# Layer-0 attention: squarings as 64x64 quadrant tiles, and the corner of the inverse made one stage early

## The reference, cut to what matters

```python
def step(Sm, inp):
    q_, k_, v_, g_, b_ = inp
    Sm = Sm * jnp.exp(g_)[..., None, None]
    kv = jnp.einsum('bhk,bhkv->bhv', k_, Sm)
    delta = (v_ - kv) * b_[..., None]
    Sm = Sm + jnp.einsum('bhk,bhv->bhkv', k_, delta)
    o = jnp.einsum('bhk,bhkv->bhv', q_, Sm)
    return (Sm, o)
```

## Time and profile before

| | |
|---|---|
| runs, us | 6044.46, 6041.1, 6032.09 (median 6041.1) |
| the profiled execution's own time, us | 6044.46 |
| span of the profile, us | 6046.2 |
| PE busy | 5221.5 us, 86% |
| DVE busy | 3480.2 us, 58% |
| ACT busy | 3055.8 us, 51% |
| POOL busy | 1178.3 us, 19% |
| squarings, L684 (five rounds of six) | 701.5 us busy on PE, 5120 records |

### The profile page before, as it was taken

One profiled execution on the slowest core, in us unless ns is written; L12 is line 12 of the kernel. 1 busy time (PEld: TensorE's weight loads), 2 busy tenths in 40 slices (PEclk: granted clock), 3 DMA queues, 4 the chain that ended last, 5 costly groups with the idle time before them and its releaser, 6 DMA issues. The chain is left out here.

```text
span 6046.2 us, 91895 instructions
## 1 busy us (share of the span) xinstructions
PE 5221.5 (86%) x32318; PEld 3893.8 (64%) x32318; DVE 3480.2 (58%) x6531; ACT 3055.8 (51%) x8923; POOL 1178.3 (19%) x1352
## 2 busy tenths in 40 slices
PE   5799999999989999989999699899998597399969
PEld 4477777877877778877887555555555354255545
DVE  3466666676666667666766566555552554543331
ACT  2466666666656666666666344344441244325421
POOL 0222222322222222222232100011110321002210
...
GB/s 85 19 19 17 13 19 19 18 17 17 19 19 13 17 19 19 17 14 19 22 19 13 46 1 1 65 1 0 0 0 20 27 1 13 21 1 1 1 21 14
DMA packets 51094, 103.57 MB, mean 17 GB/s; under 512 B 12848, under 2 KB 20176, under 8 KB 49520
## 3 DMA queue, kind: packets, MB, share of 16 engines
...
## 5 line engine op out<-in xcount | busy, mean ns | idle before, releaser
L896 ACT ACTIVATE dh_pb<-bank 64x128 f32<-64x128 f32 x3072 | 831.4, 271 | 272.5 <-PE bank L670 239.3
L684 PE MATMUL bank<-dh_cw,dh_pb 128*128 128x128 f32 x5120 | 701.5, 281 | 113.0 <-ACT dh_pb L896 111.4
L684 PEld LDWEIGHTS bank<-dh_cw,dh_pb 128*128 128x128 f32 x5120 | 635.5, 193 | 191.1 <-ACT dh_pb L896 164.4
L1034 DVE SCALAR_TENSOR_TENSOR dh_kq<-bank,dh_conv_kq,dh_kq 128x511 f32<-128x511 f32 (+2 forms) x408 | 305.4, 749 | 184.8 <-ACT dh_kq L853 173.6
L902 ACT ACTIVATE dh_cw<-bank 128x256 f32<-128x256 f32 x640 | 244.9, 385 | 255.1 <-PE bank L684 247.9
L621 PE MATMUL bank<-hT,dh_w_kq 128*128 128x512 f32 x544 | 276.7, 633 | 83.2 <-DVE dh_kq L1034 75.3
L1034 DVE SCALAR_TENSOR_TENSOR dh_v<-bank,dh_conv_v,dh_v 128x511 f32<-128x511 f32 (+2 forms) x384 | 284.2, 747 | 91.3 <-ACT dh_v L853 82.2
L1797 PE MATMUL bank<-moe_h_split,moe_w 128*128 128x512 bf16 x1200 | 277.1, 381 | 14.6 <-PEq L89 14.6
L633 PE MATMUL bank<-dh_w_vz,hT 128*128 128x256 f32 x1024 | 245.5, 383 | 22.0 <-ACT dh_zs L864 22.0
L1128 DVE TENSOR_TENSOR dh_zz<-dh_zz,bank 128x512 f32<-128x512 f32 x130 | 89.2, 686 | 283.0 <-PE bank L597 281.1
L621 PE MATMUL bank<-hT,dh_w_vz 128*128 128x512 f32 x512 | 242.5, 596 | 8.6 <-DVE dh_v L1034 8.6
...
## 6 DMA issues: line engine op xcount, KB each, us to landing
...
```

The costliest lines, as they stand in the source:

```text
L684: last = pe.matmul(square(j)[:, b, :, :], pb[j][:, b, :], src[:, :, b, :], start=True, stop=True)
L896: last = act.activation(out[half, :, o, half], src[halves[o], :, half], ACT.Copy)
L1034: dve.scalar_tensor_tensor(y, pj_bank(n)[:, 0:S - i], taps(n)[:, TAPS - 1 - i:TAPS - i], y, ALU.mult, ALU.add).then_inc(s["v_cs" if i < TA ...
```

## The change

The power and the sum are kept as pairs of 64x64 blocks for both heads at once. A block pair comes in two kinds: those whose block stays in the same half of the partitions, and those which change halves in every round. A squaring round is 16 products of 64x64 weights, two kinds times two halves of the rows, issued quadrant by quadrant; each kind writes one bank. The helpers `power`, `power_u` and `grow` serve both heads at once, with ACT copying 256 or 512 columns a time, and DVE adding in three instructions from the second round on.

The corner of the inverse is now made at the end of the stage that makes the blocks: `turn_first` turns the first block's inverse, `off_first` and `off_second` multiply it with the corner of C and with the second block's inverse, ACT copies in between, and `corner_copy` puts the result into `ttb`, which then holds the whole inverse. The recurrence uses it in one full product, `z_prod`; `w_prod`, `x_prod`, `w_copy` and `zeta` are gone. The fills are dealt out over numbered slots.

```diff
-        self.bank = [ctx.enter_context(nc.psum_tensor(f"bank{i}", [P, 512], F32)) for i in range(8)]
+        bank = lambda i, shape: ctx.enter_context(nc.psum_tensor(f"bank{i}", shape, F32))
+        first, self.pair = bank(0, [P, 512]), bank(1, [P, 2, 512])
+        self.bank = [first, self.pair[:, 0, :], self.pair[:, 1, :], *(bank(i, [P, 512]) for i in range(3, 8))]
...
+KINDS = 2
+POWERS = 6
...
-    c0 = [sb(f"c0{j}", [P, 2, NB, HALF]) for j in HEADS]
-    cw = [sb(f"cw{j}", [P, 2, NB, HALF]) for j in HEADS]
+    ttb = sb("ttb", [P, RPH, NB, P])
+    off = sb("off", [P, RPH, NB, HALF])
+    pt = sb("pt", [P, KINDS, RPH, 2, HALF])
+    c0 = sb("c0", [P, KINDS, RPH, 2, 2, HALF])
+    cw = sb("cw", [P, KINDS, RPH, 3, 2, HALF])
...
+    pair = k.pair[:, :, :].rearrange("p k (j e w n) -> p k j e w n", j=RPH, e=2, w=2)
+    both = lambda v: v.rearrange("p k j e n -> p (k j) e n")
+    turn_at = lambda g: bank[TURN][:, g * HALF:(g + 1) * HALF]
+
+    def across(kind, half):
+
+        return halves[half if kind == 0 else 1 - half]
+
...
+    def moving(i, half, kind, j, e):
+        if i == 0:
+            return c0[half, kind, j, :, e, :]
+        if i == POWERS - 1:
+            return cw[half, kind, j, 0, e, :]
+        return cw[half, kind, j, 0:2, e, :] if i % 2 else cw[half, kind, j, 1:3, e, :]
...
+    def turn_power(pe, t, i):
         if i:
+            pe.wait_ge(s["a_u"], (POWERS - 1) * t + i)
         else:
+            after(pe, s["v_u"], t)
+            after(pe, s["a_tt"], t)
+        src = cw[:, :, :, 1, :, :] if i else c0[:, :, :, 0, :, :]
+        for kind in range(KINDS):
+            for j in HEADS:
+                g = 2 * (RPH * kind + j)
+                last = pe.transpose(bank[TURN][:, g * HALF:(g + 2) * HALF],
+                                    src[:, kind, j, :, :].rearrange("p e n -> p (e n)"), k.ident[:, :])
+        last.then_inc(s["t_tr"], 1)
...
+    def square_power(pe, t, i):
         if i:
+            pe.wait_ge(s["v_w"], (POWERS - 1) * t + i)
         else:
+            after(pe, s["v_td"], t)
+        for e in range(2):
+            pe.wait_ge(s["a_pt"], 2 * POWERS * t + 2 * i + e + 1)
+            for j in HEADS:
+                at = 2 * (2 * j + e) * HALF
+                for kind in range(KINDS):
+                    for half in range(2):
+                        width = HALF if i == POWERS - 1 else 2 * HALF
+                        last = pe.matmul(bank[1 + kind][across(kind, half), at:at + width], pt[halves[half], kind, j, e, :],
+                                         moving(i, halves[half], kind, j, e), start=True, stop=True)
+        last.then_inc(s["t_sq"], 1)
...
+    def turn_first(pe, t):
+        pe.wait_ge(s["v_td"], t + 1)
+        for j in HEADS:
+            for b in range(NB):
+                last = pe.transpose(turn_at(NB * j + b), ttb[0:HALF, j, b, :], k.ident[0:HALF, 0:HALF])
+        last.then_inc(s["t_t1"], 1)
...
+    def off_first(pe, t):
+        pe.wait_ge(s["a_t1"], t + 1)
+        for j in HEADS: pe.wait_ge(hs[j]["p_nt"], t + 1)
+        for j in HEADS:
+            for g in range(2):
+                for o in range(2):
+                    last = pe.matmul(turn_at(4 + 2 * j + g)[halves[1 - o], :], off[0:HALF, j, 2 * g + o, :],
+                                     pt[0:HALF, j, g, o, :], start=True, stop=True)
+        last.then_inc(s["t_yo"], 1)
...
+    def off_second(pe, t):
+        pe.wait_ge(s["a_yo"], t + 1)
+        for j in HEADS:
+            for g in range(2):
+                for o in range(2):
+                    last = pe.matmul(turn_at(2 * j + g)[halves[o], :], pt[HALF:P, j, g, o, :],
+                                     ttb[HALF:P, j, 2 * g + o, HALF:P], start=True, stop=True)
+        last.then_inc(s["t_zo"], 1)
...
-        each(pe, B_REC[j], lambda b: ttb[j][:, b, :], lambda b: src[:, b, :]).then_inc(h["t_z"], 1)
-
-    def w_prod(pe, t, j):
-        h = hs[j]
-        pe.wait_ge(h["a_zs"], t + 1)
-        after(pe, h["p_nt"], t)
-        each(pe, B_REC[j], lambda b: ntoff[j][:, b, :], lambda b: zz[j][:, b, :]).then_inc(h["t_w"], 1)
-
-    def x_prod(pe, t, j):
-        h = hs[j]
-        pe.wait_ge(h["a_w"], t + 1)
-        each(pe, B_REC[j], lambda b: ttb[j][:, b, :], lambda b: ww[j][:, b, :]).then_inc(h["t_x"], 1)
+        each(pe, B_REC[j], lambda b: ttb[:, j, b, :], lambda b: src[:, b, :]).then_inc(h["t_z"], 1)
...
+    def power(act, t, i):
+        act.wait_ge(s["t_tr"], POWERS * t + i + 1)
+        after(act, s["t_sq"], POWERS * t + i)
+        if i == 0:
+            after(act, s["t_zo"], t)
+        src = bank[TURN][:, :].rearrange("p (g h n) -> p g h n", g=KINDS * RPH, h=2)
+        for e in range(2):
+            for half in range(2):
+                last = act.activation(pt[halves[half], :, :, e, :].rearrange("p k j n -> p (k j) n"),
+                                      src[halves[e], :, half, :], ACT.Copy)
+            last.then_inc(s["a_pt"], 1)
...
+    def power_u(act, t, i):
+        act.wait_ge(s["t_sq"], POWERS * t + i + 1)
+        act.activation(both(cw[:, :, :, 1, :, :]), both(pair[:, :, :, :, place(i, True), :]), ACT.Copy).then_inc(s["a_u"], 1)
...
+    def first_copy(act, t):
+        act.wait_ge(s["t_t1"], t + 1)
+        act.activation(pt[0:HALF, :, :, :, :].rearrange("p j g o n -> p (j g o n)"), bank[TURN][0:HALF, :], ACT.Copy)            .then_inc(s["a_t1"], 1)
...
+    def off_copy(act, t):
+        act.wait_ge(s["t_yo"], t + 1)
+        src = bank[TURN][:, 4 * HALF:8 * HALF].rearrange("p (g n) -> p g n", n=HALF)
         for o in range(2):
+            last = act.activation(pt[HALF:P, :, :, o, :].rearrange("p j g n -> p (j g) n"), src[halves[1 - o], :, :], ACT.Copy)
+        last.then_inc(s["a_yo"], 1)
...
+    def corner_copy(act, t):
+        act.wait_ge(s["t_zo"], t + 1)
+        src = bank[TURN][:, 0:4 * HALF].rearrange("p (g n) -> p g n", n=HALF)
+        out = ttb[0:HALF, :, :, HALF:P].rearrange("p j (g o) n -> p (j g) o n", o=2)
+        for o in range(2):
+            last = act.activation(out[:, :, o, :], src[halves[o], :, :], ACT.Copy)
+        last.then_inc(s["a_tt"], 1)
...
+    def start_power(dve, t):
         dve.wait_ge(s["v_kk"], order(t) + 1)
+        after(dve, s["t_sq"], POWERS * t + 1)
+        for j in HEADS:
+            dve.wait_ge(hs[j]["v_et"], order(t) + 1)
+            for half in halves:
+                split = lambda v: v[half, :, half].rearrange("p (k e) n -> p k e n", k=KINDS)
+                last = dve.tensor_tensor(c0[half, :, j, 0, :, :], split(kkm), split(et[j]), ALU.mult)
+        last.then_inc(s["v_u"], 1)
...
+    def grow(dve, t, i):
+        dve.wait_ge(s["a_u"], (POWERS - 1) * t + i + 1)
+        after(dve, s["v_w"], (POWERS - 1) * t + i)
+        to, at = product_slot(i), place(i, False)
+        if i == 0:
+            last = dve.tensor_tensor(both(cw[:, :, :, to, :, :]), both(c0[:, :, :, 1, :, :]), both(pair[:, :, :, :, at, :]),
+                                     ALU.add)
+        else:
+            old = product_slot(i - 1)
+            for half in range(2):
+                dve.tensor_tensor(cw[halves[half], 1, :, to, :, :], cw[halves[1 - half], 1, :, old, :, :],
+                                  pair[halves[half], 1, :, :, at, :], ALU.add)
+            last = dve.tensor_tensor(cw[:, 0, :, to, :, :], cw[:, 0, :, old, :, :], pair[:, 0, :, :, at, :], ALU.add)
+        last.then_inc(s["v_w"], 1)
...
+    def inverse(dve, t):
+        dve.wait_ge(s["t_sq"], POWERS * (t + 1))
+        dve.wait_ge(s["v_w"], (POWERS - 1) * (t + 1))
+        for j in HEADS: dve.wait_ge(hs[j]["t_z"], t + 1)
+        after(dve, s["t_zo"], t)
+        for half in range(2):
+            for kind in range(KINDS):
+                out = ttb[halves[half], :, 2 * kind:2 * kind + 2, halves[half]]
+                last = dve.tensor_tensor(out, cw[across(kind, half), kind, :, 0, :, :], pair[halves[half], kind, :, :, 0, :],
+                                         ALU.add)
+        last.then_inc(s["v_td"], 1)
...
-    def zeta(dve, t, j):
...
         kk_mask(dve, t)
-        for j in HEADS: normed(dve, t, j)
-        for j in HEADS: grow(dve, t, 5, j)
+        vector_fill(dve, q, a, 7)
+        for j in HEADS: decay(dve, t, j)
+        start_power(dve, t)
         qk_mask(dve, t)
-        for j in HEADS: decay(dve, t, j)
-        for j in HEADS: start_power(dve, t, j)
-        inverse(dve, t, 0)
+        normed(dve, t, 0)
+        vector_fill(dve, q, a, 8)
+        inverse(dve, t)
+        normed(dve, t, 1)
+        vector_fill(dve, q, a, 9)
         collect(dve, t)
-        inverse(dve, t, 1)
```

More of the change, by code:

```diff
@@ L678, in square_power @@
+        last.then_inc(s["t_tr"], 1)
+    def square_power(pe, t, i):
         if i:
-            pe.wait_ge(h["v_c"], 5 * t + i)
+            pe.wait_ge(s["v_w"], (POWERS - 1) * t + i)
         else:
-            after(pe, h["v_ttb"], t)
-        src = cw[j] if i else c0[j]
-        for b in range(NB):
```

(101 more changed lines are left out.)

460 lines of the change are left out of this document (207 added, 253 removed).

## The result

The changed kernel takes 6210.66 us (median of 4 runs, 6204.45 to 6227.31) against 6037.85 before: ratio 1.0286, 95% interval 1.0269 to 1.0303. Forecast were 6160 and slower. The profiled execution took 6227.31 us (span 6225.3). Its loop is nearly as steady as before's: a four of stages takes 204.8 to 205.5 us where it took 193.6 to 196.1, and 211 where it holds the loop's turn (before 200 to 201).

The account below looks back on a forecast made before the run. PE (TensorE) was taken to bound the loop: 155.9 us work, 33.4 tail waits and 7 head waits make 196.3 in four stages against 193.64, +43 in the run; with +72 for the clock, 6160 us, range 6080 to 6300.

Parts of the forecast that it names:

- PE's work: PE's busy time in four stages of layer 0's attention loop, forecast to fall from 178.25 to 155.9 us.
- The sign that was named: Listed evidence that the forecast is right: PE's busy time in four stages falls to about 156 to 160 us.
- The squarings at four quadrants: On PE, a squaring round with all four quadrants at once costs 0.89 us; 19.6 us in four stages.
- the round trip of 0.25: Changing PE's tile shape and back costs 0.25 us, nine times a stage: 9.0 us in four stages.
- The waits: PE's idle time in four stages: 33.4 us in the stage tails and 7 us in the heads.
- heads and the rest: PE's waits at the stage heads, 7 us in four stages, plus 0.4 for ACT's corner copy in the fourth.
- The clock: Long tail pauses halve PE's granted clock afterwards: three losses of 1.5 us, 4.5 in four stages, +72 in the run.
- The saving shows: Rival: shorter start products, cheaper shape changes, smaller head waits, clock 1.00; 5905 us (5850 to 6020), floor 5690; chance 0.26.
- the step that it named: In the stage's tail on DVE, head 0's norm ready about 3 us earlier, the point from which that rival decides.
- S: The end of the fifth squaring, where the stage's tail begins; tail times in us are counted from it.
- It cancels: Rival: as forecast but with clock at 1.00 and head waits at 4 us; about 6045 (6020 to 6080); chance 0.13.
- Two at a time: Rival: only two quadrants run at once in PE's squarings, a round takes 1.8 us; +285, 6445 us; chance 0.13.

Follow-up runs that it names:

- e9: e6 with PE also turning the identity, result unused, where it still waits (8, 8, 10 or 16 turns): 5651.47 us, ratio 0.935.
- e2: Changed kernel with PE turning the identity, result unused, in most of its tail waits: 6053.72 us, ratio 1.0022.
- e1: Changed kernel with query mask, both norms and inverse ahead of decays and start products on DVE: 5968.55 us, ratio 0.9888.
- e6: Changed kernel with DVE's tail and heads reordered (norms and inverse before decays) and key mask ahead of the fifth growing sum: 5727.43 us, ratio 0.949.

## Why the prediction was right, point by point

**PE's work.** Forecast 155.9 in a four, found 155.3 (e9, at clock 1.00). The sign that was named, a busy time of 156 to 160, did not come in the changed kernel itself: it is 171.1, as busy time grows with the lower clock. The squarings at four quadrants (0.89 and the change of shape) and the round trip of 0.25 both hold: a round starts 0.10 after the sixteen records ahead of it are due to end (441.26 + 16 x 0.111), and takes 1.04, 0.15 over its columns.

```profile
441.26 1.95 PE L623 MATMUL bank<-dh_S,dh_kq 128*128 128x128 f32 x16
443.14 1.10 PE L714 MATMUL bank<-dh_c,dh_pt 64*64 64x128 f32 x32
444.18 0.66 PE L628 MATMUL bank<-ident,dh_v 128*128 128x128 f32 x4
```

**The waits.** Forecast 40.4, found 33.5: mask 8.6 for 8.0, inverse 5.4 for 7.3, heads and the rest 7.1 for 7.4, norm 12.4 for 17.7. In the second stage the fifth squaring ends by 519.0; mask, first norm and inverse end at 3.7, 10.5 and 12.1 behind it, where 3.35, 10.1 and 11.8 were forecast. The norm's wait was oversized mainly for two reasons. The sixteen start products took 9.7 us, not 11.4: in the fourth stage they took 1.69 where 3.2 was forecast. They take 0.39 to 0.47 us each alone and 1.16 to 1.19 beside POOL's product `dh_inj`, which in that stage came behind them. And PE, on the lower clock, reached the turn of y later: the projection ahead of it in the third stage took 3.5 us in place of 1.73.

```profile
L1189 DVE TENSOR_TENSOR dh_c<-dh_kkm,dh_et 64x256 f32<-64x256 f32 x16 | 9.7, 608 | 0.2
```

**The clock** is the term that was mis-sized: 4.5 us in a four were forecast, from three losses of 1.5 as at the loop's turn. Found: 171.1 busy less 155.3, 15.8. (The clock's own records give much the same: PE is busy for 35.4 us at 0.50, of which half, 17.7, is the loss.) There are seven such stretches in the four, where three were counted, and not only the pauses in the tails are followed by one. In the first stage's head a projection takes 1.72 from start to next start, and the next one, behind a pause of 2.10 us, 3.43:

```profile
444.67 1.88 PE L647 MATMUL bank<-hT,dh_w_vz 128*128 128x512 f32 x4
446.39 0.60 PE L698 MATMUL bank<-ident,dh_cw 128*128 128x128 f32 x4
449.09 3.63 PE L647 MATMUL bank<-hT,dh_w_vz 128*128 128x512 f32 x4 [2.10 <-DVE dh_v L1126]
452.52 1.14 PE L623 MATMUL bank<-dh_x,dh_ttb 128*128 128x128 f32 x8
```

In the fourth stage it is low through the rest of the tail, as the w_out rows above show too:

```profile
630.20:643.11 12.91, 12.10 (x65) 8.94 (x63) 2.36 (x4) 3.30 (x7) 3.28 (x4) 0.50 0.05 18
```

e2 shows it as a cause: with the tail's pauses filled the four is 194.48, close to the 196.3 that the sum had without the clock.

**The sum.** 155.3 + 33.5 + 15.8 = 204.6, the measured four 204.80, where 200.8 was forecast with the clock. The clock's 11.3 too few and the waits' 6.9 too many pull in opposite directions; that the forecast came within 1% of 6211 is to that extent luck. Not all of the time is the loop's: of the 179 us by which the profiled spans differ, 167 have come about by the end of layer 0's attention, and 12 lie behind it, which no run here explains.

**The rivals.** "The saving shows" was one reordering on DVE away: e1 took the step that it named (in the second stage the first norm ends at S + 6.3 in place of 10.5) and came out 1.1% under the kernel before; e6 reached 5727, near that rival's floor of 5690, and e9, in which PE waits less than in the kernel before, 5651. "It cancels" named about 6045 with the clock at 1.00; e2 comes near it with 6054. "Two at a time" is refuted by 1.04 us a round and by the records that start in fours, and with it the rule of the Trainium skill ("TensorEngine Tiling (Array Packing)", Gotcha 1) in the reading that this rival took: quadrants of different rows that write different partitions of one bank ran together here, and the measurement decides.
